# Gate logits folded into the K and output projections as extra columns, biases of K, V and output on TensorE, the expert split divided between ScalarE and VectorE, and the attention loop with a new order

## The reference

```python
h = concat([tok(x), txt], axis=1)                       # 64 x 114 x 256
h = h + attn(layernorm(h));  h = h + ffn(layernorm(h))
# attn: Q = elu(x Wq + bq) + 1, K = elu(x Wk + bk) + 1, V = x Wv + bv, 16 heads of 16
KV = einsum('bshd,bshe->bhde', K, V); Z = 1 / (einsum('bshd,bhd->bsh', Q, K.sum(1)) + 1e-6)
out = einsum('bshd,bhde,bsh->bshe', Q, KV, Z) @ Wo.T + bo
# ffn: 8 experts, one per token
logits = x @ gate_w.T; sel = argmax(logits); rw = sigmoid(max(logits)); xs = x * rw
out = (xs @ w_up[sel].T) * silu(xs @ w_gate[sel].T) @ w_down[sel].T
```

## Time and profile before

| what | value |
|---|---|
| median of 3 runs | 539.52 us (536.44 to 542.34) |
| profiled execution | 540.68 us, span 538.9 us |
| mean granted TensorE clock | 0.946 of full speed |
| busy, share of span: TensorE, VectorE, ScalarE, GpSimd | 89%, 73%, 61%, 61% |
| patches stage | to about 52 us |
| attention and routing | to about 420 us |
| experts | from 424 us to the end |

### The profile page before, as it was taken

How to read it: one execution, slowest core, us unless ns; L and a number is a source line. 1 busy time by engine, 2 the same in 40 slices (tenths; PEclk the granted TensorE clock), 3 DMA queues, 4 the chain that set the end, 5 groups by cost and what they waited for, 6 DMA issues and landing times. The chain is left out here.

```text
span 538.9 us, 12682 instructions
## 1 busy us (share of the span) xinstructions
PE 477.9 (89%) x3604; PEld 442.2 (82%) x3604; DVE 395.4 (73%) x1327; ACT 326.1 (61%) x784; POOL 326.5 (61%) x689
## 2 busy tenths in 40 slices
PE   5998889969999999999899899999975299999991
PEld 5998678858998998999888888998974299899991
DVE  4585567557888888888776787988772379889881
ACT  4454366445666676677566665677532388788870
POOL 0023233544766767767887778667667157678874
PEclk9999899969999999999998998999995599999996
DMA  8762111110211226211111111100111667772220
GB/s 271 241 220 63 49 49 50 55 43 27 61 31 31 61 84 212 59 31 32 43 49 29 31 31 44 53 24 19 33 35 42 177 182 223 210 225 87 83 83 32
DMA packets 34933, 45.85 MB, mean 85 GB/s; under 512 B 9133, under 2 KB 27040, under 8 KB 34868
## 3 DMA queue, kind: packets, MB, share of 16 engines
q1 hardware_dynamic: 24980, 29.41, 18.6%
q0 software_dynamic: 9216, 15.12, 9.0%
q10 hardware_dynamic: 672, 0.53, 0.3%
HBM read 26.30 MB, written 17.17 MB: 81 GB/s over the span
## 5 line engine op out<-in xcount | busy, mean ns | idle before, releaser
L580 POOL DMA_INDIRECT sorted_rows<-rows,place x64 | 74.9, 1171 | 39.6 <-POOL place L575 28.6
L651 POOL DMA_INDIRECT out<-result,result_id x64 | 62.6, 979 | 26.7 <-DVE result L1132 12.3
L726 ACT ACTIVATE k_neg<-k_in 114x512 f32<-114x512 f32 x32 | 20.2, 633 | 70.5 <-DVE k_in L1026 70.5
L554 POOL TENSOR_SCALAR ve<-mv 114x2 f32<-114x2 f32 x64 | 15.2, 237 | 71.3 <-issue 47.1
L1151 PE MATMUL b_kvp<-wkv_hi,xnT_hi 128*114 128x512 f32 x128 | 54.6, 427 | 0.0
L1152 PE MATMUL b_kvp<-wkv_lo,xnT_hi 128*114 128x512 f32 x128 | 51.4, 401 | 0.0
L1153 PE MATMUL b_kvp<-wkv_hi,xnT_lo 128*114 128x512 f32 x128 | 51.3, 401 | 0.0
L557 POOL TENSOR_TENSOR rstd<-ve,half_neg 114x2 f32<-114x2 f32 x64 | 46.3, 724 | 5.3
L602 POOL TENSOR_TENSOR k_sb<-k_exp,k_relu 114x512 f32<-114x512 f32 x32 | 41.1, 1284 | 11.6 <-issue 10.4
L738 ACT ACTIVATE xn<-rows_all,shift,rstd 114x256 f32<-114x256 f32 x64 | 34.9, 592 | 21.6 <-issue 19.3
L1151 PE MATMUL b_qo<-xnT_hi,wq_hi 128*128 128x256 f32 x128 | 39.5, 308 | 6.3 <-DVE rows L938 6.3
(11 more groups left out here) (187 smaller groups left out, 1736.6 us busy)
## 6 DMA issues: line engine op xcount, KB each, us to landing
rows_all<-sorted_rows SPq DMA_DIRECT2D x64, 130.0 KB
rows_all<-in_x SPq DMA_DIRECT2D x18, 384.0 KB, 4.1
rows_all<-in_txt SPq DMA_DIRECT2D x32, 154.0 KB
rows_all<-in_wgu SPq DMA_DIRECT2D x8, 256.0 KB, 4.6
rows_all<-patch_out SPq DMA_DIRECT2D x48, 36.0 KB
sorted_rows<-rows,place POOLq DMA_INDIRECT x64, 3.7
rows_all<-in_wdown SPq DMA_DIRECT2D x8, 128.0 KB, 4.7
out<-result,result_id POOLq DMA_INDIRECT x64
```

What stands on the lines that cost most here:

```text
L580: G.indirect_dma_start(out=scratch[0:EXPERTS * REGION, :], out_offset=bass.IndirectOffsetOnAxis(ap=place[:, k, b:b + 1], axis=0), in_=rows ...
L651: G.indirect_dma_start(out=out, out_offset=bass.IndirectOffsetOnAxis(ap=result_id[:, k:k + 1], axis=0), in_=result[:, k, :], in_offset=Non ...
```

## The change

- The 8 gate columns are centred (the mean over features is taken out) and appended to Wk: the K product of the first normalised tokens becomes 264 wide and also gives a gate part. The product Wo x gate, made on the chip, is appended to Wo as 8 columns. The gate logits, up to a positive factor per token, are then the output projection's 8 extra columns times the first inverse deviation plus the gate part. The second normalisation, its turn, its copy and the gate product go. The factor (`ratio`) is applied on GpSimd to the top value alone.
- Biases of K, V and output are products of a row of ones with bias rows (33 rows, high part in one and low part in the last) that open each accumulation. K and V go to separate banks and separate products: 2 x (1 + 6) of 264 columns and 2 x (1 + 6) of 256. K's bias row has 1 added, so ScalarE takes one exponential (bias -1) and VectorE one minimum and maximum for the map.
- ScalarE copies V and the denominators out of the banks. GpSimd no longer makes the K sum.
- The low parts of gate and up weights are subtracted by VectorE one step after ScalarE's high parts; those of down in steps 27 to 30.
- `ROW_SETS` has sets of three pairs from pair 6 on, each followed by one text load. Weight loads come earlier on SyncE, the split of weights later.
- The order of the steps is new on every engine; the first normalisation is one pair ahead instead of two, the draining steps are written out, and the banks are allotted anew.

```diff
-ROW_SETS = [range(0, 1), range(1, 2), range(2, 3), range(3, 4), range(4, 8), range(8, 16), range(16, 24), range(24, 32)]
+ROW_SETS = [range(0, 1), range(1, 2), range(2, 3), range(3, 4), range(4, 6), *(range(n, min(n + 3, 32)) for n in range(6, 32, 3))]
...
+            for n in range(6, EXPERTS_AT):
+                if n < len(ROW_SETS):
+                    patch_rows(n)
                 load_text(n)
...
+            def project(p):
+
+                k_, tokens = p % 2, [slice(b * TOK, (b + 1) * TOK) for b in range(2)]
...
+                for b in range(2):
+                    to = b_kg[0:TOK, b, 0:KGW]
+                    T.matmul(to, ones_r[:], bias_r[:, BIAS_K:BIAS_V], start=True, stop=False)
+                    for k in range(KC):
+                        last = product(to, (xnT_hi[:, k_, k, tokens[b]], xnT_lo[:, k_, k, tokens[b]]),
+                                       (wkgv_hi[:, k, 0:KGW], wkgv_lo[:, k, 0:KGW]), False, k == KC - 1)
+                last.then_inc(kg_done, 1)
...
+                for b in range(2):
+                    to = b_v[0:TOK, b * D:(b + 1) * D]
+                    T.matmul(to, ones_r[:], bias_r[:, BIAS_V:], start=True, stop=False)
...
+            def queries(p):
+
+                if p >= 2:
+                    pe.wait_ge(logits_ready, p - 1)
...
+                V.scalar_tensor_tensor(k_sb[:], k_exp[:], 1.0, b_kg[0:TOK, :, 0:D], ALU.min, ALU.max).then_inc(k_ready, 1)
...
+            def gate_logits(p):
+
+                dve.wait_ge(wo_done, p + 1)
+                dve.wait_ge(gate_part_ready, p + 1)
+                for b in range(2):
+                    last = V.scalar_tensor_tensor(logits[:, p % 2, b, :], b_w[0:TOK, b, D:KGW], rstd1[:, p % 8, b:b + 1],
+                                                  gate_part[:, p % 4, b, :], ALU.mult, ALU.add)
+                last.then_inc(logits_ready, 1)
```

The new order of TensorE and of VectorE in a step:

```diff
+                if 0 <= i - 4:
+                    rank(i - 4)
+                if 0 <= i - 1:
+                    key_value(i - 1)
+                if 0 <= i - 2:
+                    turn_attention(i - 2)
+                if 0 <= i:
+                    project(i)
+                if 0 <= i - 2:
+                    project_out(i - 2)
+                if 0 <= i - 1:
+                    apply(i - 1)
+                if 0 <= i + 1 < PAIRS:
+                    turn_tokens(i + 1)
+                if 0 <= i:
+                    queries(i)
...
+                if 0 <= i - 1:
+                    masked(i - 1)
+                if 0 <= i - 4:
+                    places(i - 4)
+                if 0 <= i - 2:
+                    attention_low(i - 2)
+                if 0 <= i - 1:
+                    queries(i - 1)
+                if 0 <= i + 2 < PAIRS:
+                    stats_1(i + 2)
+                if GU_STEP < i <= GU_STEP + EXPERTS:
+                    gate_up_low(i - GU_STEP - 1)
+                if DOWN_STEP < i <= DOWN_STEP + EXPERTS // 2:
+                    down_low(i - DOWN_STEP - 1)
+                if 0 <= i - 3:
+                    route(i - 3)
+                if 0 <= i:
+                    keys(i)
+                if 0 <= i - 2:
+                    residual(i - 2)
+                    gate_logits(i - 2)
+                if 0 <= i - 1:
+                    attention(i - 1)
+                if 0 <= i + 1 < PAIRS:
+                    tokens_low(i + 1)
+                if 0 <= i - 2:
+                    stats_2(i - 2)
```

The weights' preparation between the patch units, on TensorE and on VectorE:

```diff
+            units(pe, unit, [0, 1, 2, lambda: pe.wait_ge(posb_ready, 2), *range(3, 9), gate_centre, 9, 10, gate_weights,
+                             *range(11, 17), lambda: early_step(-1), 17])
...
+                position, lambda: w_tok_part(0), 0, lambda: w_tok_part(1), 1, 2, 3, 4, 5, tables, *range(6, 10),
+                gate_centred, 10, 11, gate_columns, 12, lambda: weight_low(0), 13, lambda: weight_low(1), lambda: step(-2), 14,
+                lambda: weight_low(2), 15, 16, 17, lambda: step(-1), room_setup])
```

## The result

The changed kernel takes 564.83 us (median of 4, 563.93 to 566.42) beside 540.93 for the kernel before: ratio 1.0447, 95% interval 1.0403 to 1.0492. It is 4.5% slower, where 498 us was forecast, range 486 to 514. The profiled execution has a span of 562.1 us at a mean granted clock of 0.964.

What follows compares the result with a forecast made beforehand. TensorE alone was taken to bound ordinary steps of 10.16 us. 73.0 + 29 x 9.5 + 0.5 = 349.0 against 389.32, -40.3; drain -1; so 540.68 - 41.3 = 499.4, as median 498 us, range 486 to 514.

Steps and rivals of the forecast that it cites:

- pair 0's residual: VectorE's residual addition for the first pair of images, marking the end of start-up: forecast at 73.0 us against 76.25 before.
- pairs 0 to 29, with the split: 29 attention steps of 9.5 us plus 0.5, including steps where VectorE also subtracts for the experts' weight split.
- The upper bound of 10.1: TensorE's attention step if every one of the 42 projection products cost the queries' 0.132 us: 10.1 us.
- the third: Rival, 5%: narrow K and V products pay for exposed weight loads, 16 more per step, 56 us, ending at 554.
- TensorE's step without that term: Ordinary attention step, set by TensorE alone: forecast to fall from 10.06 us by its rows to 9.5.
- The rival of waits (15%): Freed TensorE time turns into waits, as at banks shared by queries and output projection; step near 10.05, 514 us; 15%.
- The first stall: Pairs 0 to 4: 9.4 us lost as VectorE waits for a text load queued behind SyncE's patch copies; would go.
- Late loads (5%): Rival, 5%: SyncE's patch copies remain ahead of need, so the first stall stays: 507 us.
- The second stall: Pairs 17 to 29: 9.1 us lost as GpSimd's 1.3 us gate/up subtraction overfills its step; would go.
- The +0.5 for VectorE's tight steps: Expert-split steps: subtractions moved to VectorE use up its slack before the residual, adding 0.5 us in all.
- The start: Work before the first key product: +2 us, to 53.8, for folding weights and new small operations; bounds 0 and +5.
- The drain: Last steps, from pair 29's residual to the expert stage: 1 us shorter, bounds -4 and +4.

Runs made afterwards that it cites:

- the kernel of 128 rows: The changed kernel with its six bias products per pair padded with zeros from 33 to 128 rows, same result: 492.49 us, ratio 0.9115 to the kernel before.

## Why the prediction was wrong

It had the wrong sign through one term of its sum, the price of the bias products. The terms in us, with the kernel of 128 rows as the change without the mis-sized one:

| term | forecast | after | 128 rows |
|---|---|---|---|
| pair 0's residual | 73.0 | 77.66 | 72.67 |
| one step | 9.5 | 11.63 | 9.41 |
| pairs 0 to 29, with the split | 276.0 | 337.2 | 272.7 |
| pair 29 to SyncE's start of the expert stage | 33.7 | 33.25 | 30.3 |
| expert stage | 114.9 | 114.0 | 114.0 |
| span | 497.6 | 562.1 | 489.7 |

- **The step that failed** is "No row shows a bias product of 33 rows in this type", with the bounds put on it. I took 0.119 or 0.116 for each, as for its neighbours; measured, a bias product and what it does to its neighbours takes 0.50 (the ordinary 0.12 and 0.38). The upper bound of 10.1 was the nearest row, 0.132, times all 42 products. But every row, its bias product too, has 114 or 128 rows. They bound the price of such products and say nothing of an alternation with 33 rows, which the attention loop of before had nowhere. The kernel before's own bias product was 128 rows high though it needs only three; the change made it 33. I named the height and yet priced it by type and width alone.
- **The rival that came nearest** is the third, given 5%: "bias products of 33 rows between others of 128" stood there as what was left for it. Its price was laid on the wrong products. The 16 products more per step are not what pays: in the kernel of 128 rows they stand 0.12 apart, loads hidden, and the step is 9.41. Six changes of rows pay, 0.38 each. Its result of 554 was near by chance, and so was its sign: K and V take 4.84 us per step (209.69 to 214.53), over the 4.2 that I had set, but by four such changes, and 3.45 with 128 rows.
- **A rule I passed over** is in the Trainium skill, TensorEngine Tiling (Array Packing), Key Properties: a change of tiling mode (among which it counts 64 or 32 rows instead of 128) "drains the TensorE". The runs agree with it: 0.38 us there and back, with the boundary between 64 and 65 rows. The page gives no price and doesn't say that a product with few rows changes the mode by itself; that the cost measured here is this drain is the likeliest reading, but no run shows it. The rule I did weigh, on weight loads, is not borne out by either kernel: between products of 128 rows, loads for the same rows start a product ahead, 0.12 apart.
- **TensorE's step without that term** was right: 9.41 against 9.5, and it is TensorE's alone, as forecast. The rival of waits (15%) is refuted at this step: without bias products it goes to 8.68 with no gap. Its wait for the logits does appear in the split of that run, at a step of 9.08.
- **The first stall** went, for the reason given: no wait for text is left, and the order of SyncE alone makes the old kernel 9.3 us faster. I took all of it for a queue; 4.9 of its 10.8 us were TensorE at a lower clock behind the wait. Late loads (5%) are refuted.
- **The second stall** went, but the reason was part of the truth. When GpSimd's subtraction is moved, 7.0 of 9.1 us go and 2.1 stay, and 3.1 of the 7.0 are clock. In the changed kernel the move earns nothing; whether because the K sum had left GpSimd or because the gate product had left TensorE is open. The +0.5 for VectorE's tight steps did not come.
- **The start** was right (72.67 against 73.0; first key product of the kernel after at 53.74, forecast 53.8). In the kernel after 14 bias products add 5.0.
- **The drain** was under-rated: 30.3 in place of 33.7, a gain of 4.4 where I gave 1, just past my bound of 4. What shortened it, no run shows. In the kernel after, 2.9 of it is lost to the bias products of the last steps.

## What to carry to other kernels

Before a new operand shape is priced by its neighbours, compare every dimension of it with the rows that give the price; where one differs (here the rows of the stationary operand), that is the unknown, and rows which all share the other value bound nothing. A product of 33 to 64 rows in a stream of full ones was cheapest when padded with zeros to more than 64 rows; putting it next to its like saves a part. And when a kernel gets slower with TensorE busy 100% at granted clock 1.00, look at the distances between the starts of successive products around each change of shape before looking at waits. A stall is also more than its idle time: read the granted clock behind it.

## What the runs showed of the hardware

- A change of TensorE from products of 128 rows to one of 33 or 64 rows and back costs 0.38 us at granted clock 1.00 in fp32r, 0.33 for a bf16 product between fp32r ones. 33 and 64 rows cost the same; 65 rows cost nothing beside 128 (9.44 and 9.41 us per step). In the rows read, loads of weights don't run ahead across such a change. Why, the trace doesn't show.
- A "busy" of 100% hides it: the rows of the products at the change grow from 0.28 to 0.37 and close up, so that the page counts the loss as work.
- In the kernel before, the granted clock is at 0.50 (1.2 GHz) from 113 to 122 us, at and behind the end of an idle piece of TensorE of 5.57 us, and for some 3 us each, 1 to 2 us behind two idle pieces of 1.04 and 1.00 us. Behind two longer ones, 1.36 us until 262.62 and 1.50 us until 307.79, it stays at 1.00. So the same idle time can cost much or nothing: 6.5 us idle came with a mean clock of 0.90 in one execution and 0.96 in another. Whether the idle time causes the drops wasn't tried by itself.
- On one chip the same kernel took 28 us longer from pair 31's residual to the end (155.6 instead of 127.4), nearly all of it in the expert stage, at attention steps equal to a hundredth. The stage table of it shows 117 GB/s there instead of 143 and a granted clock of 0.90 instead of 0.88; the cause stays open.
